# GpSimd adds the halves of each head before VectorE sums them in a softmax attention

## The chip, the cores and the metric

The kernel runs on one core of one Trainium2 chip. The metric is the device time of one execution in microseconds (us); lower is better. The engines are TensorE (PE; PEld is its weight load), VectorE (DVE), ScalarE (ACT), GpSimd (POOL) and SyncE (SP, here only a DMA queue). Each runs its own queue in order, and the queues meet at semaphores.

## The reference

Two attention layers, each followed by a feed-forward part with routed experts, on an input of 4 sequences of 512 rows of 256 values. The change lies in the second attention, a softmax over 64 keys in 16 heads:

```python
q = (Q @ Wq_w + Wq_b).reshape(b, tq, H, DK).transpose(0, 2, 1, 3)
scores = jnp.einsum('bhqd,bhkd->bhqk', q, k) / jnp.sqrt(jnp.float32(DK))
scores = jnp.where(mask == 0, jnp.float32(-1000000000.0), scores)
attn = jax.nn.softmax(scores, axis=-1)
out = jnp.einsum('bhqk,bhkd->bhqd', attn, v)
return out.transpose(0, 2, 1, 3).reshape(b, tq, c) @ Wo_w + Wo_b
```

Everything is float32. The layer norm ahead of it, and the routing and experts behind it, are part of the same kernel.

## The kernel before

The function `softmax_attention` runs from about 430 to 628 us of the span. The 2048 query rows are 16 tiles (n = 0 to 15) of 128 rows, four for each sequence b. One tile's scores are 128 x 1024 numbers (16 heads of 64 keys) in `s_sc`, a ring of three buffers. A hand-written schedule of 27 ticks sets the order on every engine; tick n works on these tiles:

- TensorE: `probs_T(n-2)` transposes the finished probabilities (L1045), then `scores(n+1)` (L50 to L52 with kz) computes the next scores, then what a remainder r = n mod 4 adds: the query projection `q_proj`, the output projection `project`, router logits, transposes of inputs.
- VectorE: `bounded(n)` copies the scores out of PSUM under the mask (L898) and takes each head's maximum (L904). Then `reciprocals(n-1)` sums the exponentials of each head (L910, 1024 columns to 16) and inverts the sums (L912). Then come the extras of r: layer-norm work (L877, L859 and the small chain of L83 to L88), low halves of the split numbers (L884, L890, L993), the residual (L917).
- GpSimd: its loop (L760 to L768) has in iteration n the subtraction of the maximum from tile n (L763), then the multiplication of tile n-1 by its reciprocals (L767).
- ScalarE: the exponential of tile n-1 (L829), the copy of the transposed tile n-2 (L835), and the extras of r: L794 (high half of the queries), L826 (high half of the attention output), L776 (layer norm), L787 (high half of a transposed input).

So the way of one tile n is: scores, L898, L904, L763, L829, L910, L912, L767, L1045, L835. In PE's queue, `scores(n+1)` stands behind `probs_T(n-2)`, and `bounded(n+1)` needs these scores and `probs_T(n-2)`. At tick 16 TensorE's queue holds `probs_T(14)`, `project(2)`, which waits for the transposed input of sequence 1 (L884, behind L787, behind L835), and from there on a row of products: the shared expert's first layer, logits, its second layer, and so on to about 628 us, where all engines leave the function together. Extras that are queued once a sequence on ScalarE stand ahead of the exponential when r is 1 or 3 (L794, L826).

Of the kernel before, what the change touches and what calls it, by code (L numbers as in the profile page):

```python
# [10 lines left out]
ALU = mybir.AluOpType  # L11
ACT = mybir.ActivationFunctionType
AX = mybir.AxisListType

B, S, D = 4, 512, 256
KEYS = 64
HEADS = 16
HD = D // HEADS
P = 128
T = B * S  # L20
NT = T // P
# [649 lines left out]
def softmax_attention(nc, k, io):  # L671
# [11 lines left out]
    with ctx:  # L683
        def sb(name, shape, dt=F32):
            return ctx.enter_context(nc.sbuf_tensor(f"s_{name}", shape, dt))

        def sem(name):
            return ctx.enter_context(nc.semaphore(f"s_{name}"))
# [14 lines left out]
        sc = sb("sc", [P, 3, HEADS, KEYS])  # L703
        top = sb("top", [P, 2, HEADS])
        pT = sb("pT", [P, PAIRS, S])
        den, rden = sb("den", [P, 2, HEADS]), sb("rden", [P, 2, HEADS])

        u32 = xq
# [9 lines left out]
        q_done, qh_ok, ql_ok = sem("q_done"), sem("qh_ok"), sem("ql_ok")  # L718
        s_done, cl_ok, mx_ok, sub_ok, p_ok, den_ok, sum_ok, nm_ok = (
            sem(n) for n in ("s_done", "cl_ok", "mx_ok", "sub_ok", "p_ok", "den_ok", "sum_ok", "nm_ok"))  # L720
        pt_done, pc_ok, pv_done, oh_ok, ol_ok = (sem(n) for n in ("pt_done", "pc_ok", "pv_done", "oh_ok", "ol_ok"))
        y_done, y_used, lg_done, lg_ok = (sem(n) for n in ("y_done", "y_used", "lg_done", "lg_ok"))
        fb_ld, f1_ld, f2_ld = sem("fb_ld"), [sem(f"f1_ld{h}") for h in range(2)], [sem(f"f2_ld{h}") for h in range(2)]
# [9 lines left out]
        @block.sync  # L733
        def _(sp):
            for h in range(2):
                sp.dma_start(f32(sw1_lo(h)), k["fw"][0, E1, :, h * FH:(h + 1) * FH]).then_inc(f1_ld[h], 16)
            sp.wait_ge(bo0, 1)
            sp.dma_start(bo[0:1, :], io["bo"]).then_inc(c_ld, 16)
            sp.dma_start(mask_i[:], io["mask"]).then_inc(c_ld, 16)
            sp.dma_start(rw[:], io["rw"][1]).then_inc(c_ld, 16)  # L740
            sp.dma_start(bq[:], io["bq"]).then_inc(fb_ld, 16)
            sp.dma_start(k["fb1"][:], io["fb1"]).then_inc(fb_ld, 16)

            sp.wait_ge(s_done, NT // 2)
            for h in range(2):
                sp.dma_start(f32(sw2_lo(h)), k["fw"][1, E1, :, h * FH:(h + 1) * FH]).then_inc(f2_ld[h], 16)

        @block.gpsimd
        def _(pool):
            def gather(b):  # L750
                for t in range(b * TB, (b + 1) * TB):
                    pool.indirect_dma_start(out=k["xn"][:, t, :], out_offset=None, in_=k["ys0"],
                                            in_offset=bass.IndirectOffsetOnAxis(ap=k["back0"][:, t:t + 1], axis=0)).then_inc(yg_ok[b], 16)

            gather(0)
            nc.gpsimd.memset(bo[:], 0.0).then_inc(bo0, 1)
            gather(1)
            gather(2)
            gather(3)
            for n in range(NT + 1):  # L760
                if n < NT:
                    pool.wait_ge(mx_ok, n + 1)
                    nc.gpsimd.tensor_tensor(sc[:, n % 3], sc[:, n % 3], top[:, n % 2, :, None].to_broadcast([P, HEADS, KEYS]),  # L763
                                            ALU.subtract).then_inc(sub_ok, 1)
                if 1 <= n < NT + 1:
                    pool.wait_ge(sum_ok, n)
                    nc.gpsimd.tensor_tensor(sc[:, (n - 1) % 3], sc[:, (n - 1) % 3],  # L767
                                            rden[:, (n - 1) % 2, :, None].to_broadcast([P, HEADS, KEYS]), ALU.mult).then_inc(nm_ok, 1)  # L768
# [86 lines left out]
        def _(dve):  # L855
# [48 lines left out]
                nc.vector.tensor_reduce(top[:, n % 2], sc[:, n % 3], AX.X, ALU.max).then_inc(mx_ok, 1)  # L904

            def reciprocals(n):
                dve.wait_ge(p_ok, n + 1)
                if n >= 2:
                    dve.wait_ge(nm_ok, n - 1)
                nc.vector.tensor_reduce(den[:, n % 2], sc[:, n % 3], AX.X, ALU.add).then_inc(den_ok, 1)  # L910
                dve.wait_ge(den_ok, n + 1)
                nc.vector.reciprocal(rden[:, n % 2], den[:, n % 2]).then_inc(sum_ok, 1)  # L912

# [53 lines left out]
            for n in range(TICKS):  # L967
# [3 lines left out]
                if 1 <= n < NT + 1:  # L971
                    reciprocals(n - 1)
# [1064 lines left out]
def build(nc, io, out):  # L2037
    ctx = ExitStack()
    with ctx:
# [45 lines left out]
        k["sw1_hi"], k["sw1_lo"] = (lambda h: sw1_hi[:, h]), (lambda h: sw1_lo[:, h])  # L2085
        k["sw2_hi"], k["sw2_lo"] = (lambda h: keys[:, B // 2 + h]), (lambda h: keys[:, h])
        softmax_attention(nc, k, io)
        last_ffn_phase(nc, k, io, out)

# [56 lines left out]
```

## Time and profile before

| | us |
|---|---|
| median of 3 runs | 827.67 (826.83 to 831.08) |
| the profiled execution | 825.63 |
| its span in the trace | 824.2 |

| engine | busy us | share of the span |
|---|---|---|
| TensorE (PE) | 670.3 | 81% |
| VectorE (DVE) | 524.8 | 64% |
| ScalarE (ACT) | 337.0 | 41% |
| GpSimd (POOL) | 209.0 | 25% |

Busy shares are averages over stages with different limits. In a timeline row the first two numbers are the start and the duration in us; the bracket, where there is one, is the idle time of that engine just before the instruction and what ended it.

### The profile page before, as it was taken

How to read it: one execution, taken by the hardware profiler on the slowest of the kernel's cores; microseconds unless marked ns; L12 is line 12 of the kernel's file. 1: busy time of each engine (PE TensorE's matmuls, PEld its weight loads, DVE VectorE, ACT ScalarE, POOL GpSimd, SP SyncE). 2: the span in 40 equal slices, each digit the busy share in tenths (PEclk: the TensorE clock that was granted, in tenths of full speed). 3: DMA queues.
4: the chain of work that ended last, by engine and by line, in shares of the span. 5: the costliest groups of instructions: out<-in, count | busy, mean ns of one | idle time of the engine just before them, and what ended most of it. 6: DMA issues, size and time to landing. Idle time of an engine off the chain costs nothing. (4 is left out here: it accounts for less than half of the span.)

```text
span 824.2 us, 15063 instructions
## 1 busy us (share of the span) xinstructions
PE 670.3 (81%) x4947; PEld 613.4 (74%) x4948; DVE 524.8 (64%) x1322; ACT 337.0 (41%) x555; POOL 209.0 (25%) x324
## 2 busy tenths in 40 slices
PE   4898825989999989998606578677897789999996
PEld 3566525889999989998505456457797789999995
DVE  6855645777445885447557888886545675565556
ACT  7544354554334563335522544444322433343321
POOL 7533250000000000000063565550001711011161
PEclk9999956999999999999857779898998999999998
DMA  7999126655100449200141001000004411111124
GB/s 268 419 417 392 74 94 242 210 159 177 59 25 25 137 176 358 92 25 13 33 128 32 1 0 52 1 0 1 1 1 151 168 48 38 39 51 51 35 74 135
DMA packets 22997, 90.71 MB, mean 110 GB/s; under 512 B 4401, under 2 KB 8754, under 8 KB 17362
## 3 DMA queue, kind: packets, MB, share of 16 engines
q1 hardware_dynamic: 15794, 68.64, 22.4%
q0 software_dynamic: 7168, 21.63, 8.7%
q8 instruction: 18, 0.29, 0.1%
q14 instruction: 17, 0.14, 0.1%
HBM read 50.94 MB, written 45.61 MB: 117 GB/s over the span
## 5 line engine op out<-in xcount | busy, mean ns | idle before, releaser
L1469 ACT ACTIVATE e_h<-psum,e_be 128x256 f32<-128x256 f32 x144 | 67.7, 475 | 141.8 <-PE psum L52 140.2
L50 PE MATMUL psum<-e_h_hi,e_w_hi 128*128 128x256 f32 x384 | 110.2, 287 | 6.2 <-DVE e_w_lo L1560 5.5
L51 PE MATMUL psum<-e_h_lo,e_w_hi 128*128 128x256 f32 x384 | 107.9, 281 | 0.0
L52 PE MATMUL psum<-e_h_hi,e_w_lo 128*128 128x256 f32 x384 | 107.8, 281 | 0.0
L1866 ACT ACTIVATE vz<-psum,fb 128x256 f32<-128x256 f32 x112 | 52.4, 474 | 108.3 <-PE psum L52 105.0
L1552 DVE CAST e_h_hi<-e_h 128x256 fp32r<-128x256 f32 x144 | 43.5, 302 | 82.6 <-ACT e_h L1469 82.6
L50 PEld LDWEIGHTS psum<-e_h_hi,e_w_hi 128*128 128x128 f32 x384 | 72.3, 188 | 9.7 <-DVE e_w_lo L1560 8.8
L52 PEld LDWEIGHTS psum<-e_h_hi,e_w_lo 128*128 128x128 f32 x384 | 72.4, 188 | 0.0
L51 PEld LDWEIGHTS psum<-e_h_lo,e_w_hi 128*128 128x128 f32 x384 | 72.3, 188 | 0.0
L1554 DVE TENSOR_TENSOR e_h_lo<-e_h,e_h_hi 128x256 fp32r<-128x256 f32 x144 | 61.3, 426 | 4.9
L50 PE MATMUL psum<-e_gT_hi,e_w_hi 128*128 128x256 f32 x192 | 55.5, 289 | 9.4 <-DVE e_w_lo L1627 7.8
L52 PE MATMUL psum<-e_gT_hi,e_w_lo 128*128 128x256 f32 x192 | 54.7, 285 | 0.0
L51 PE MATMUL psum<-e_gT_lo,e_w_hi 128*128 128x256 f32 x192 | 54.7, 285 | 0.0
L1915 DVE TENSOR_TENSOR f_h_lo<-vz,f_h_hi 128x256 fp32r<-128x256 f32 x112 | 47.7, 426 | 3.8
L50 PEld LDWEIGHTS psum<-e_gT_hi,e_w_hi 128*128 128x128 f32 x192 | 37.1, 193 | 10.8 <-issue 10.8
L1913 DVE CAST f_h_hi<-vz 128x256 fp32r<-128x256 f32 x112 | 33.2, 297 | 17.7 <-ACT vz L1866 16.4
L763 POOL TENSOR_TENSOR s_sc<-s_sc,s_top 128x1024 f32<-128x1024 f32 x16 | 30.4, 1903 | 55.0 <-DVE s_top L904 54.9
L50 PE MATMUL psum<-kz_hi,s_qT_hi 128*128 128x256 f32 (+1 forms) x80 | 32.5, 407 | 13.8 <-DVE s_sc L898 9.8
L50 PE MATMUL psum<-f_gT_hi,f_w_hi 128*128 128x256 f32 x144 | 40.2, 279 | 0.0
L50 PE MATMUL psum<-xT_hi,sw_hi 128*128 128x256 f32 (+1 forms) x128 | 38.2, 298 | 2.5 <-issue 1.3
L51 PE MATMUL psum<-f_gT_lo,f_w_hi 128*128 128x256 f32 x144 | 40.2, 279 | 0.0
L52 PE MATMUL psum<-f_gT_hi,f_w_lo 128*128 128x256 f32 x144 | 40.2, 279 | 0.0
(410 smaller groups left out, 2129.8 us busy)
## 6 DMA issues: line engine op xcount, KB each, us to landing
xs<-zeros SPq DMA_DIRECT2D x18, 1024.0 KB
e_w_raw<-in_W SPq DMA_DIRECT2D x18, 1024.0 KB, 5.2
ys<-zeros SPq DMA_DIRECT2D x6, 1024.0 KB
ys<-e_yo POOLq DMA_DIRECT2D x14, 256.0 KB, 3.7
e_xg<-xs POOLq DMA_DIRECT2D x13, 256.0 KB, 6.8
e_w_raw<-in_W SPq DMA_DIRECT2D x6, 512.0 KB, 8.0
f_w_lo<-fw SPq DMA_DIRECT2D x6, 512.0 KB
ys<-x_norm POOLq DMA_DIRECT2D x10, 256.0 KB, 2.6
```

What stands on the lines that cost most here:

```text
L50: nc.tensor.matmul(out, wh, xh, start=start, stop=False)
L51: nc.tensor.matmul(out, wh, xl, start=False, stop=False)
L52: return nc.tensor.matmul(out, wl, xh, start=False, stop=stop)
L763: nc.gpsimd.tensor_tensor(sc[:, n % 3], sc[:, n % 3], top[:, n % 2, :, None].to_broadcast([P, HEADS, KEYS]), ALU.subtract).then_inc(sub_ok, 1)
L1469: nc.scalar.activation(h32[:, m % RING], ps[:, HIDDEN_BANKS[m % RING], 0:SLOT], ACT.Gelu, bias=be[:, m:m + 1]).then_inc(gelu_ok, 1)
L1552: nc.vector.tensor_copy(h_hi[:, m], h32[:, m % RING]).then_inc(hh_ok, 1)
L1554: nc.vector.tensor_tensor(h_lo[:, m], h32[:, m % RING], f32(h_hi[:, m]), ALU.subtract).then_inc(hl_ok, 1)
L1866: nc.scalar.activation(h32[:, m % RING], ps[:, HIDDEN_BANKS[m % RING], 0:SLOT], ACT.Relu, bias=b1[:, f * MH + m:f * MH + m + 1]).then_inc( ...
L1913: nc.vector.tensor_copy(h_hi[:, m], h32[:, m % RING]).then_inc(hh_ok, 1)
L1915: nc.vector.tensor_tensor(h_lo[:, m], h32[:, m % RING], f32(h_hi[:, m]), ALU.subtract).then_inc(hl_ok, 1)
```

## The change

A buffer `pairs` (128 x 16 x 32) and a semaphore `add_ok` are new. In the GpSimd loop, iteration n first waits for the exponential of tile n-1 and adds the two halves of 32 keys of each head into `pairs` (512 columns out of twice 512); from n = 2 on it also waits until VectorE has read `pairs` of the tile before (`den_ok`). Only then come the subtraction of tile n and the multiplication of tile n-1, as before. VectorE's sum waits for that addition in place of the exponential, and reads 512 columns of `pairs` in place of 1024 of `s_sc`.

```diff
+        pairs = sb("pairs", [P, HEADS, KEYS // 2])
...
+        add_ok = sem("add_ok")
...
             for n in range(NT + 1):
+
+                if 1 <= n < NT + 1:
+                    pool.wait_ge(p_ok, n)
+                    if n >= 2:
+                        pool.wait_ge(den_ok, n - 1)
+                    p = sc[:, (n - 1) % 3]
+                    nc.gpsimd.tensor_tensor(pairs[:], p[:, :, 0:KEYS // 2], p[:, :, KEYS // 2:KEYS], ALU.add).then_inc(add_ok, 1)
                 if n < NT:
                     pool.wait_ge(mx_ok, n + 1)
                     nc.gpsimd.tensor_tensor(sc[:, n % 3], sc[:, n % 3], top[:, n % 2, :, None].to_broadcast([P, HEADS, KEYS]),
...
             def reciprocals(n):
-                dve.wait_ge(p_ok, n + 1)
+                dve.wait_ge(add_ok, n + 1)
                 if n >= 2:
                     dve.wait_ge(nm_ok, n - 1)
-                nc.vector.tensor_reduce(den[:, n % 2], sc[:, n % 3], AX.X, ALU.add).then_inc(den_ok, 1)
+                nc.vector.tensor_reduce(den[:, n % 2], pairs[:], AX.X, ALU.add).then_inc(den_ok, 1)
```

## Rows read from the trace of the kernel before

**Rows 1.** The page, busy us, share of the span and instruction count of each engine:

```profile
PE 670.3 (81%) x4947; PEld 613.4 (74%) x4948; DVE 524.8 (64%) x1322; ACT 337.0 (41%) x555; POOL 209.0 (25%) x324
```

**Rows 2.** Stretches of the span: length, busy us of PE, PEld, DVE, ACT, POOL; clock; DMA:

```profile
440.00:560.00 120.00, 83.84 (x432) 62.37 (x430) 100.11 (x180) 54.75 (x69) 61.34 (x32) 0.83 0.03 9
560.00:628.00 68.00, 60.87 (x464) 57.97 (x464) 36.15 (x106) 20.41 (x37) 0.00 (x0) 0.92 0.00 1
```

**Rows 3.** Groups in 440 to 560 us: busy us, mean ns | idle before, its releasers:

```profile
L898 DVE SCALAR_TENSOR_TENSOR s_sc<-psum,s_cap 128x1024 f32<-128x1024 f32 x16 | 19.5, 1222 | 7.5 <-PE psum L52 7.4
L910 DVE TENSOR_REDUCE s_den<-s_sc 128x16 f32<-128x1024 f32 x16 | 19.4, 1210 | 4.2 <-ACT s_sc L829 4.2
...
L767 POOL TENSOR_TENSOR s_sc<-s_sc,s_rden 128x1024 f32<-128x1024 f32 x16 | 31.4, 1965 | 4.0 <-DVE s_rden L912 4.0
L763 POOL TENSOR_TENSOR s_sc<-s_sc,s_top 128x1024 f32<-128x1024 f32 x16 | 30.4, 1903 | 55.0 <-DVE s_top L904 54.9
```

**Rows 4.** Groups of the whole span that have nearby sizes, same columns:

```profile
L1608 DVE TENSOR_REDUCE e_r_gone<-e_r_after 128x16 f32<-128x128 f32 x1 | 0.3, 288 | 0.0
...
L66 POOL TENSOR_TENSOR a_ln_tmp<-a_ln_tmp,a_ln_half 128x4 f32<-128x4 f32 x9 | 1.8, 199 | 0.7
...
L1442 POOL MEMSET e_yo<- 128x512 f32 x1 | 0.5, 522 | 0.0
```

**Rows 5.** Timeline, ticks 1 to 3, VectorE, TensorE and GpSimd:

```profile
459.81 1.21 DVE L910 TENSOR_REDUCE s_den<-s_sc 128x16 f32<-128x1024 f32 x1
459.98 1.90 POOL L763 TENSOR_TENSOR s_sc<-s_sc,s_top 128x1024 f32<-128x1024 f32 x1 [8.10 <-DVE s_top L904]
...
461.84 1.90 POOL L767 TENSOR_TENSOR s_sc<-s_sc,s_rden 128x1024 f32<-128x1024 f32 x1
...
462.46 1.21 DVE L898 SCALAR_TENSOR_TENSOR s_sc<-psum,s_cap 128x1024 f32<-128x1024 f32 x1
...
463.79 1.97 PE L1045 MATMUL psum<-ident,s_sc 128*128 128x128 f32 x8 [2.17 <-POOL s_sc L767]
...
468.36 1.22 DVE L898 SCALAR_TENSOR_TENSOR s_sc<-psum,s_cap 128x1024 f32<-128x1024 f32 x1 [2.02 <-PE psum L52]
```

**Rows 6.** Timeline, ticks 9 and 10, GpSimd, ScalarE and VectorE:

```profile
507.05 1.91 POOL L763 TENSOR_TENSOR s_sc<-s_sc,s_top 128x1024 f32<-128x1024 f32 x1
...
507.95 1.27 ACT L794 ACTIVATE s_qT_hi<-psum,s_bq 128x512 fp32r<-128x512 f32 x2 [4.82 <-PE psum L52]
509.11 1.06 ACT L829 ACTIVATE s_sc<-s_sc 128x1024 f32<-128x1024 f32 x1
...
510.20 1.22 DVE L910 TENSOR_REDUCE s_den<-s_sc 128x16 f32<-128x1024 f32 x1 [3.23 <-ACT s_sc L829]
...
513.50 1.05 ACT L829 ACTIVATE s_sc<-s_sc 128x1024 f32<-128x1024 f32 x1
```

**Rows 7.** Timeline, ticks 15 and 16, from the last exponentials to `project(2)`:

```profile
551.32 1.05 ACT L829 ACTIVATE s_sc<-s_sc 128x1024 f32<-128x1024 f32 x1
551.48 1.90 POOL L763 TENSOR_TENSOR s_sc<-s_sc,s_top 128x1024 f32<-128x1024 f32 x1 [1.24 <-DVE s_top L904]
...
552.40 1.22 DVE L910 TENSOR_REDUCE s_den<-s_sc 128x16 f32<-128x1024 f32 x1 [0.99 <-ACT s_sc L829]
...
553.98 1.90 POOL L767 TENSOR_TENSOR s_sc<-s_sc,s_rden 128x1024 f32<-128x1024 f32 x1 [0.60 <-DVE s_rden L912]
...
555.94 1.09 PE L1045 MATMUL psum<-ident,s_sc 128*128 128x128 f32 x8 [3.68 <-POOL s_sc L767]
...
557.99 1.02 ACT L787 ACTIVATE xT_hi<-psum 128x1024 fp32r<-128x1024 f32 x1
...
559.04 1.23 DVE L884 TENSOR_TENSOR xT_lo<-psum,xT_hi 128x1024 fp32r<-128x1024 f32 x1 [2.65 <-ACT xT_hi L787]
...
560.37 0.55 PE L50 MATMUL psum<-s_w_hi,s_oT_hi 128*128 128x256 f32 x1 [3.33 <-issue]
```

**Rows 8.** Timeline, GpSimd's one long multiplication:

```profile
477.65 2.88 POOL L767 TENSOR_TENSOR s_sc<-s_sc,s_rden 128x1024 f32<-128x1024 f32 x1
```

## The prediction

> **What bounds the kernel now.** I read the page first: TensorE is busy for 81% of the span, VectorE 64%, GpSimd 25% [rows 1]. These averages hide the stage that is touched, so next came the stretches [rows 2]. From 440 to 560 us, where the 16 softmax tiles run, VectorE is busy 100.1 of 120 us, TensorE 83.8 and GpSimd 61.3. From 560 to 628 us, the rest of the function, VectorE has 36 of 68 us and TensorE 60.9. So only the first stretch can pay for less VectorE work, and it pays only up to the instruction that opens the second: `project(2)` on TensorE at 560.37 [rows 7]. From there TensorE's queue runs one fixed row of products with short waits, and all engines leave together, so a shift of that start passes on one for one.
>
> Inside the stretch the groups tell who makes VectorE wait [rows 3]: 7.4 us before its L898 for scores from TensorE, and 4.2 us before its L910 for the exponential. GpSimd stood idle for 55 us before its subtractions, waiting for VectorE's maximum, and 4.0 us before its multiplications. It looks like a free engine beside a full one. The timeline has to say where each is late.
>
> **The change part by part.** The sum is walked through the queues: each instruction starts at the later of its queue coming free and its last input being done plus 0.03 us; durations are those of the trace. For the kernel before, this walk lands `project(2)` at 560.18, where the trace has 560.37, so it is good to about 0.2 us; differences are better.
>
> *The shorter sum.* L910 takes 1210 ns for 1024 columns [rows 3], and a reduction of 128 columns into 16 takes 288 ns [rows 4]. The slope is (1210 - 288) / 896 = 1.03 ns a column, so 512 columns take 288 + 384 x 1.03 = 683 ns. VectorE saves 0.53 us a tile, 8.5 us over 16 tiles. The bound from the other side is no saving at all (the fixed cost or the layout eats it).
>
> *The added addition.* No row shows this operation. GpSimd's two-input operation takes 199 ns for 4 columns [rows 4] and 1903 ns for 1024 [rows 3]: slope 1.67 ns, so 512 columns take 199 + 508 x 1.67 = 1048 ns. I take 1.05 us. From below, a memset of 512 columns, which reads nothing, takes 0.52 us [rows 4]; from above, the subtraction of 1024 columns takes 1.90 us, since both halves together are 1024 numbers read and the large row reads one of its operands broadcast. The row nearest in kind and form is the two-input operation, hence the value from its slope.
>
> The Trainium skill, "GPSIMD Engine Reference", section "Elementwise — side-by-side cycle accounting", gives 4497 ns for a two-input add of 2048 columns; a quarter of it is an estimate of 1.12 us, and with it the sum below would end 0.2 us later. The same page's section on engine selection says to leave elementwise work and sums along the free dimension to VectorE. By it the move costs more than it frees, and the rows here agree (1.05 us spent for 0.53 us freed); whether that shows in the time depends on who is waiting.
>
> *The moved waits.* The addition stands at the head of the iteration, so behind its wait for the exponential of tile n-1 are queued the subtraction of tile n (for which the exponential n waits on ScalarE, and through it everything after) and the multiplication n-1 (for which TensorE waits). The wait for `den_ok` of the tile before costs nothing: that sum is over before the multiplication that stands ahead in GpSimd's own queue.
>
> Now tick by tick, times against before:
>
> - Ticks 1 to 3. `bounded(2)` at 462.46 follows back to back behind the sum of 459.81 and comes 0.53 earlier. `bounded(3)` at 468.36 waited 2.02 us for TensorE, whose queue had `probs_T(0)` first, which waited for the multiplication of tile 0 [rows 5]. That multiplication starts when the subtraction gives GpSimd free (459.98, then 461.84, 1.86 later), so it does not move, and neither does `bounded(3)`. Gain 0.
> - Ticks 4 to 8. VectorE is the late one at ticks 5 and 6: `bounded(5)` comes 0.51 earlier and `bounded(6)` 1.04. From there TensorE's scores set the pace, moved by the same. GpSimd's iteration is now 1.01 + 1.86 + 1.86 = 4.73 us, against some 3.4 of VectorE in a tick without extras (L898, L904 and the sum at 1.22, 1.22 and 0.68, and a short inversion), and just fits in ticks that have extras or a wait for scores. Gain 1.1 at `bounded(8)`.
> - Ticks 9 and 10. ScalarE has L794 ahead of the exponential of tile 8, at 509.11, and VectorE waits 3.23 us for it [rows 6]. All this comes 1.08 earlier, but the addition (1.05 + 0.03) stands between: the sum starts at 510.21, where it was. Only its own 0.53 is left as gain. The subtraction of tile 9, at 507.05 before [rows 6], now starts at 510.1; its exponential ran only at 513.50 [rows 6], behind other work of ScalarE, which covers this delay of 3 us; were that cover gone, tick 10 would be 3 us later.
> - Ticks 11 to 15. Nothing more is won, since scores and extras set the pace: `bounded(15)` and the exponential of tile 14 come 0.53 earlier.
> - The exit. The exponential of tile 14 ends at 552.37 in the trace [rows 7], now at 551.84. The addition runs 551.87 to 552.92. Before, the subtraction of tile 15 ran from 551.48, beside this exponential; now it stands behind the addition and starts at 552.88. The multiplication of tile 14 waits for GpSimd and starts at 552.88 + 1.86 = 554.74, though its reciprocal is ready at about 553.9. Before, it started at 553.98 [rows 7]: 0.76 later. Behind it come L1045, L835, L787, L884 and `project(2)`, each released by the one before [rows 7], with nothing to absorb the delay.
>
> Sum: 0.53 earlier turned into 0.8 later (0.81 in the walk) at `project(2)`. The profiled execution (825.63, 1.4 us more than its span of 824.2) would go to 826.4, and the median of 827.67 to **828.5**.
>
> Bounds in the same walk: an addition of 0.52 us gives -0.3; 1.27 us gives +1.6; 1.90 us gives +4.9. An unshortened sum with the addition of 1.05 gives +2.6.
>
> **The rivals.**
>
> *GpSimd becomes the loop (slower).* If the addition costs near the large row's 1.90 us, GpSimd's iteration is 3 x 1.86 = 5.6 us. Then the add and subtraction are late in the ticks around 5, 10, 12 and 13 too, and the walk ends 4.9 us later: 832.6. It decides from about 1.1 us on: up to there only the exit is lost, above it each further 0.1 us costs 0.4 to 0.5. For it: both inputs are full tensors, unlike any row. One multiplication took 2.88 in place of 1.90 us, beside VectorE's L877 [rows 8], so a neighbour can stretch GpSimd. Against it: L877 runs twice in all, and no addition falls beside it. The skill's page "GPSIMD Engine Reference", section "Specifications", names VectorE instructions with two SBUF inputs as contenders, and L877 is one; by it the additions, which lie beside others, would not be stretched.
>
> *The gain stays (faster).* If TensorE's scores were early in most ticks, 0.53 would be kept in each: 8.5 less the 1.3 lost at the exit, 7.2 us faster, 820.5. For it: VectorE is busy 83% of the stretch. Against it: the waits of [rows 3] and the two places above where nothing is kept.
>
> *The sum does not get shorter.* Then 1.21 us of VectorE stays, and the time is 827.67 + 2.6 = 830.3.
>
> *The clock.* TensorE's granted clock averages 0.83 in the first stretch and 0.92 in the second [rows 2], so stretches at 1.2 GHz lie among those at 2.4 GHz. In the second, which is TensorE's, 0.92 means 2 x 0.08 x 68 = 10.9 us at the lower level. The shift can make that a third more or less: 3.6 us at half speed, 1.8 us of time either way, at this size still within 0.5%.
>
> **How the numbers follow.** The forecast has 0.75 (no change that can be measured; about 0.5%, 4.1 us, is what a measurement of this kernel can tell from none), GpSimd as the loop 0.09 (slower), the gain that stays 0.05 (faster), the unshortened sum 0.03 (no change), the clock by more than 1.8 us 0.08 (0.01 faster, 0.02 slower, the rest no change). That makes 0.06 faster, 0.83 the same, 0.11 slower. The range reaches down by the clock and the short addition to 826.0, and up to the dear addition, 832.6.
>
> **What would show each step.** The sum at L910's place near 0.68 us; the new addition near 1.05 us and 16 times; `bounded(3)` unmoved; the subtraction of tile 9 about 3 us later with nothing waiting; VectorE's idle time before its sum grown, released by GpSimd; at the exit the order addition, subtraction, multiplication back to back, and `project(2)` 0.8 us later. An addition above 1.3 us, or scores that arrive early in ticks 3 and 11 to 15, would make the prediction wrong.

## The result, and the profile after

The changed kernel takes 839.12 us (median of 4 executions, 837.94 to 841.33) against 828.04 for the kernel before in the same comparison: ratio 1.0126, 95% interval 1.0092 to 1.016, so 11.1 us slower. Forecast was 828.5, no change that can be measured, in a range of 826.0 to 832.6. The profiled execution took 841.33 us and has a span of 839.9.

The stretches say where the time went. The cuts lie at four events: the first L898 of tile 0 (L907 in the changed kernel), the start of `project(2)`, the end of the function's last logits, and the first transposed routed slot of the next function. First the kernel before, then the changed one; the columns are those of rows 2.

```profile
447.40:560.37 112.97, 79.50 (x423) 59.39 (x421) 95.43 (x168) 51.90 (x63) 61.34 (x32) 0.83 0.03 10
560.37:628.20 67.83, 61.07 (x464) 58.05 (x464) 35.78 (x105) 20.04 (x37) 0.00 (x0) 0.92 0.00 1
628.20:673.52 45.32, 34.48 (x247) 32.49 (x247) 32.31 (x81) 15.42 (x26) 22.54 (x36) 0.89 0.46 166
673.52:824.20 150.68, 141.38 (x1190) 139.51 (x1188) 87.79 (x243) 50.27 (x105) 28.69 (x34) 0.99 0.19 58
```

```profile
450.06:568.14 118.08, 83.57 (x422) 63.95 (x421) 89.84 (x168) 52.02 (x63) 80.89 (x48) 0.79 0.03 10
568.14:641.39 73.25, 66.49 (x464) 63.45 (x464) 35.75 (x105) 20.09 (x37) 0.00 (x0) 0.85 0.00 1
641.39:689.38 47.99, 34.47 (x247) 32.55 (x247) 32.32 (x81) 15.07 (x26) 20.76 (x36) 0.86 0.43 157
689.38:839.90 150.52, 140.66 (x1190) 139.65 (x1188) 88.18 (x243) 50.45 (x105) 28.81 (x34) 0.99 0.19 58
```

The 16 ticks take 5.1 us more. The part behind `project(2)` takes 5.4 us more with the same 464 matmuls: TensorE's busy time there grows by all of it (61.07 to 66.49 us, with 6.76 us idle in both), and its granted clock is 0.85 in place of 0.92. The next function takes 2.7 us more and the part ahead of the ticks 2.7 us (450.06 against 447.40); neither holds changed code, and the first experiment takes both out.

Inside the ticks, the groups that answer to rows 3 (busy us, mean ns | idle before, its releasers):

```profile
L776 POOL TENSOR_TENSOR s_sc<-s_sc,s_rden 128x1024 f32<-128x1024 f32 x16 | 31.5, 1967 | 1.1 <-DVE s_rden L921 1.1
L772 POOL TENSOR_TENSOR s_sc<-s_sc,s_top 128x1024 f32<-128x1024 f32 x16 | 30.5, 1906 | 28.5 <-DVE s_top L913 28.5
L769 POOL TENSOR_TENSOR s_pairs<-s_sc 128x512 f32<-128x512 f32 x16 | 20.4, 1274 | 16.1 <-ACT s_sc L838 16.1
...
L907 DVE SCALAR_TENSOR_TENSOR s_sc<-psum,s_cap 128x1024 f32<-128x1024 f32 x16 | 19.5, 1221 | 8.8 <-PE psum L52 8.6
...
L919 DVE TENSOR_REDUCE s_den<-s_pairs 128x16 f32<-128x512 f32 x16 | 10.9, 682 | 12.5 <-POOL s_pairs L769 12.3
```

VectorE's sum fell from 1210 to 682 ns, as worked out (683). That frees 8.5 us, but VectorE now waits 12.3 us for the addition, where it waited 4.2 us for the exponential [rows 3]. The addition takes 1.27 us, not 1.05, and GpSimd itself waits 16.1 us for exponentials with the next subtraction queued behind.

Tick 0 shows something the prediction did not have (timeline of VectorE and of GpSimd):

```profile
459.09 0.16 DVE L87 SCALAR_TENSOR_TENSOR s_ln_rstd<-s_ln_tmp,s_ln_rstd 128x4 f32<-128x4 f32 x1
459.29 1.10 DVE L85 TENSOR_TENSOR s_ln_tmp<-s_ln_rstd 128x4 f32<-128x4 f32 x1
460.43 0.16 DVE L86 TENSOR_TENSOR s_ln_tmp<-s_ln_tmp,s_ln_half 128x4 f32<-128x4 f32 x1
...
459.12 1.25 POOL L769 TENSOR_TENSOR s_pairs<-s_sc 128x512 f32<-128x512 f32 x1 [4.59 <-ACT s_sc L838]
```

One operation of 4 columns in the layer-norm chain takes 1.10 us in place of 0.16, and ends 0.02 us after the addition beside it. In tick 13 the same happens to an operation with one input, 1.04 us in place of 0.17. In that tick VectorE also waits 2.12 us for `project(1)`, where it waited 0.33 before; `project(1)` begins at 538.20, and from there TensorE has no pause until tile 15's scores are done at 554.45:

```profile
546.68 1.27 POOL L769 TENSOR_TENSOR s_pairs<-s_sc 128x512 f32<-128x512 f32 x1 [2.32 <-ACT s_sc L838]
546.93 1.04 DVE L875 TENSOR_SCALAR s_ln_var<-s_ln_mv 128x4 f32<-128x4 f32 x1
...
543.76 1.28 DVE L926 SCALAR_TENSOR_TENSOR x_res<-psum,tg,x_res 128x1024 f32<-128x1024 f32 x1 [2.12 <-PE psum L1074]
...
538.20 0.35 PE L50 MATMUL psum<-s_w_hi,s_oT_hi 128*128 128x256 f32 x1 [1.94 <-issue]
```

The tick that answers to rows 6 (ScalarE, GpSimd, VectorE) and the exit that answers to rows 7:

```profile
512.12 1.06 ACT L838 ACTIVATE s_sc<-s_sc 128x1024 f32<-128x1024 f32 x1
513.25 1.28 POOL L769 TENSOR_TENSOR s_pairs<-s_sc 128x512 f32<-128x512 f32 x1 [3.50 <-ACT s_sc L838]
514.49 1.90 POOL L772 TENSOR_TENSOR s_sc<-s_sc,s_top 128x1024 f32<-128x1024 f32 x1
514.57 0.69 DVE L919 TENSOR_REDUCE s_den<-s_pairs 128x16 f32<-128x512 f32 x1 [4.44 <-POOL s_pairs L769]
...
556.84 1.04 ACT L838 ACTIVATE s_sc<-s_sc 128x1024 f32<-128x1024 f32 x1
557.96 1.27 POOL L769 TENSOR_TENSOR s_pairs<-s_sc 128x512 f32<-128x512 f32 x1 [1.25 <-ACT s_sc L838]
559.19 1.91 POOL L772 TENSOR_TENSOR s_sc<-s_sc,s_top 128x1024 f32<-128x1024 f32 x1
559.27 0.69 DVE L919 TENSOR_REDUCE s_den<-s_pairs 128x16 f32<-128x512 f32 x1 [2.29 <-POOL s_pairs L769]
559.99 0.25 DVE L921 RECIPROCAL s_rden<-s_den 128x16 f32<-128x16 f32 x1
...
561.05 1.90 POOL L776 TENSOR_TENSOR s_sc<-s_sc,s_rden 128x1024 f32<-128x1024 f32 x1
...
563.01 1.80 PE L1054 MATMUL psum<-ident,s_sc 128*128 128x128 f32 x8 [2.81 <-POOL s_sc L776]
568.14 0.55 PE L50 MATMUL psum<-s_w_hi,s_oT_hi 128*128 128x256 f32 x1 [3.33 <-issue]
```

The queue order is the forecast one: addition, subtraction, multiplication, back to back, with the reciprocal ready at 560.24, 0.8 us before GpSimd takes it.

Counted from tile 0's L898, these are the starts of the L898 of some tiles, and of `project(2)`:

| | tile 1 | 2 | 3 | 6 | 9 | 10 | 12 | 14 | 15 | project(2) |
|---|---|---|---|---|---|---|---|---|---|---|
| before | 10.02 | 15.06 | 20.96 | 40.88 | 57.09 | 71.20 | 81.00 | 96.52 | 101.52 | 112.97 |
| changed | 10.96 | 15.47 | 21.57 | 41.05 | 57.59 | 72.38 | 83.01 | 100.32 | 104.43 | 118.08 |
| difference | +0.94 | +0.41 | +0.61 | +0.17 | +0.50 | +1.18 | +2.01 | +3.80 | +2.91 | +5.11 |

### The profile page after: what moved, and what is told of

It is laid out like the page before. It is cut to its first block and busy times, and to the rows that moved or that the text cites. A ratio compares the mean times of both kernels' runs of the same rounds, so it can differ in the third digit from the quotient of the medians.

```text
span 839.9 us, 15094 instructions
## 1 busy us (share of the span) xinstructions
PE 681.5 (81%) x4947; PEld 626.4 (75%) x4948; DVE 519.1 (62%) x1322; ACT 337.1 (40%) x555; POOL 227.2 (27%) x340
## 5 line engine op out<-in xcount | busy, mean ns | idle before, releaser
L1478 ACT ACTIVATE e_h<-psum,e_be 128x256 f32<-128x256 f32 x144 | 67.8, 475 | 141.9 <-PE psum L52 140.3
L50 PE MATMUL psum<-e_h_hi,e_w_hi 128*128 128x256 f32 x384 | 110.3, 287 | 6.2 <-DVE e_w_lo L1569 5.5
L50 PEld LDWEIGHTS psum<-e_h_hi,e_w_hi 128*128 128x128 f32 x384 | 72.3, 188 | 9.7 <-DVE e_w_lo L1569 8.8
L50 PE MATMUL psum<-e_gT_hi,e_w_hi 128*128 128x256 f32 x192 | 55.5, 289 | 9.4 <-DVE e_w_lo L1636 7.8
L50 PE MATMUL psum<-kz_hi,s_qT_hi 128*128 128x256 f32 (+1 forms) x80 | 33.6, 420 | 15.6 <-DVE s_sc L907 11.5
L50 PEld LDWEIGHTS psum<-e_gT_hi,e_w_hi 128*128 128x128 f32 x192 | 37.2, 194 | 10.8 <-issue 10.8
L50 PE MATMUL psum<-f_gT_hi,f_w_hi 128*128 128x256 f32 x144 | 40.2, 279 | 0.0
L50 PE MATMUL psum<-xT_hi,sw_hi 128*128 128x256 f32 (+1 forms) x128 | 37.9, 296 | 1.1 <-issue 1.1
```

What stands on the lines that cost most here:

```text
L50: nc.tensor.matmul(out, wh, xh, start=start, stop=False)
L1478: nc.scalar.activation(h32[:, m % RING], ps[:, HIDDEN_BANKS[m % RING], 0:SLOT], ACT.Gelu, bias=be[:, m:m + 1]).then_inc(gelu_ok, 1)
```

## The experiments

Each time is given as a ratio to the kernel before, timed beside it on the same chip, with its 95% interval, since the kernel before itself has medians from 822.4 to 828.0 us in these comparisons. "Ticks" is the stretch from the first L898 to `project(2)`, "behind" the stretch from there to the function's end; 113.0 and 67.8 in the kernel before.

**Both kernels again.** No edit. Are the parts outside the ticks the change's?

> The kernel before once more, unchanged, for a second profile of it. The change as the cause of everything: bounded(0) again near 447.4 us, 113.0 us from there to project(2), 67.8 us from there to the end of the function, granted clock 0.92, total within 2 us of 828. Chance as the cause of the parts outside the 16 ticks (in the changed kernel's profile 2.7 us before the first tile, 5.5 us behind project(2) and 2.7 us in the next function): one of these parts comes out longer here too, by 2 us or more.

> The changed kernel once more, unchanged. If its queues are the cause: 118.0 us again from bounded(0) to project(2), within 0.5, and the 5.5 us behind project(2) again, since the same idle stretch of TensorE is ahead of it; 2.7 us before the first tile gone if that was chance. If the clock of TensorE falls by chance: behind project(2) anything between 68 and 74 us.

The kernel before again: ratio 1.0006 (0.9986 to 1.0027), ticks 112.99, behind 67.85. The changed kernel again: 1.0132 (1.0093 to 1.017), ticks 118.07, behind 73.81, next function 43.2 us in both. So the next function's 2.7 us were chance. The first tile starts anywhere from 447.3 to 451.7 us over 16 profiles of kernels of either kind (451.7 in one without any addition), so that difference is chance too. The 5.1 and the 5.4 to 6.0 us repeat, and together are the 11 us.

**The gain alone.** VectorE sums 512 columns of a constant tile, no addition.

```diff
-nc.vector.tensor_reduce(den[:, n % 2], sc[:, n % 3], AX.X, ALU.add)
+nc.vector.tensor_reduce(den[:, n % 2], pairs[:], AX.X, ALU.add)   # kernel before; pairs is filled once with 1.0
```

> Leaves out the addition on GpSimd: VectorE sums 512 columns of a constant tile in place of the 1024 exponentials of a tile, with the waits of the kernel before, so the probabilities are not normalised. It is the gain alone. The walk through the queues: bounded(6) 1.1 us earlier, bounded(10) 1.6 us, project(2) 2.2 us earlier: 110.8 us for the stretch, and the total 2 us below before (0.3 per cent). The rival, that VectorE's busy time is the bound and 16 x 0.53 us are worth their full 8.5 us: 819.5 us.

Ratio 0.9976 (0.9954 to 0.9999), ticks 109.8: 3.2 us off the ticks and 2.1 us off the median. The walk had 2.2. The rest is TensorE's clock: its product of the probabilities with the values behind the scores of tile 6 took 2.83 us in place of 3.64, and `q_proj` behind those of tile 9 took 2.74 in place of 3.67. So 8.5 us of VectorE's time were worth 3.2 here, even at no cost.

**The cost alone.** The addition as in the changed kernel, but VectorE sums the 1024 columns and waits for the exponential; GpSimd waits for its own additions, which keeps `s_sc` safe.

```diff
-pool.wait_ge(den_ok, n - 1)
+pool.wait_ge(add_ok, n - 1)
...
+pool.wait_ge(add_ok, n)        # ahead of the multiplication
...
-dve.wait_ge(add_ok, n + 1)
+dve.wait_ge(p_ok, n + 1)
...
-nc.vector.tensor_reduce(den[:, n % 2], pairs[:], AX.X, ALU.add)
+nc.vector.tensor_reduce(den[:, n % 2], sc[:, n % 3], AX.X, ALU.add)
```

> The addition runs on GpSimd as in the changed kernel, but nobody uses it: VectorE sums the 1024 exponentials itself and does not wait for the addition. It is the cost alone. If an addition of 1.27 us only fills GpSimd's queue: the walk gives project(2) 1.7 us later (114.7 us for the stretch). If besides it shuts VectorE out of small two-input operations while it runs, as one of them that took 1.10 instead of 0.16 us in the profile of the changed kernel suggests: 1 us more for each of the layer-norm chains that an addition meets (two of them there), 116.5 us. The total 3 to 9 us above before, the rest of it TensorE's clock.

> The kernel with an addition that nobody uses, unchanged. Its profiled execution took 824.7 and its four timed ones 834.6 to 836.4. If the clock behind project(2) has two outcomes for the same instructions, this profile may show the other: stretch 116.3 again, and 73 to 79 us behind project(2) in an execution of 835. If the stretch itself differs by 5 us or more, the two outcomes lie inside the 16 ticks.

Ticks 116.3 and 115.6. The walk had 114.7 for the queue alone and 116.5 with two waits of the kind seen in tick 0 (the lock, see below), so the first profile is near the second value and the other one midway. The first tick takes 10.96 in both, that is, 0.94 longer, though no one waits for the addition. Ratios 1.0157 (1.0121 to 1.0193) and 1.0082 (1.0047 to 1.0117): the executions of these identical kernels spread from 822.7 to 836.4 us. Both profiles are of quick ones (824.7 and 822.7) with 67.9 and 68.2 behind, so which stretch holds the 10 us of the others was not seen.

**The form of the addition, and the lock.** A kernel of its own: GpSimd runs an operation twice, alone or beside 20 VectorE operations of 4 columns (or 5 sums of 512, or 4 copies of 256).

> A kernel of its own that leaves out the whole computation: it copies its input to its output, and beside that GpSimd runs pairs of one operation alone, then beside small VectorE operations. Form of the addition: if the strided halves are the cause of 1.27 us, the flat 512-column addition takes about 1.05; if two full operands are, all of them take 1.27 and the one with a broadcast operand about 1.05. Lock: if a GpSimd operation with two inputs shuts out VectorE operations with two SBUF inputs until it ends, some 128x4 operations of VectorE show up to 1.3 us in place of 0.16 beside the additions, and none beside a GpSimd memset or where VectorE reads one input, or one from PSUM. If it is a plain share of bandwidth, all kinds get a little longer and none waits for the end.

GpSimd's groups (busy us, mean ns; L38 is the addition of strided halves, L42 flat operands, L45 and L53 a broadcast second operand, L50 two full ones):

```profile
L38 POOL TENSOR_TENSOR g_o<-g_a 128x512 f32<-128x512 f32 x12 | 14.9, 1261 | 7.4 <-DVEq L115 7.1
...
L53 POOL TENSOR_TENSOR g_o<-g_a,g_s 128x1024 f32<-128x1024 f32 x4 | 7.5, 1906 | 0.3
...
L50 POOL TENSOR_TENSOR g_o<-g_a,g_b 128x1024 f32<-128x1024 f32 x2 | 4.6, 2337 | 0.1
...
L42 POOL TENSOR_TENSOR g_o<-g_a,g_b 128x512 f32<-128x512 f32 x2 | 2.5, 1260 | 0.1
L45 POOL TENSOR_TENSOR g_o<-g_a,g_s 128x512 f32<-128x512 f32 x2 | 2.0, 1046 | 0.1
```

The form of the halves costs nothing (1261 against 1260). The broadcast operand is what made the large row cheap: 512 columns with one take 1046 ns, which is to 2 ns the price that the prediction took from such a row.

VectorE's operations (count, then minimum / median / maximum ns): beside additions, two SBUF inputs (L68), one SBUF input (L71), one from PSUM (L74), sums of 512 (L77), copies of 256 (L81); then L68 again beside a GpSimd operation with one input, beside a memset, and beside the broadcast subtraction:

```profile
L68 DVE TENSOR_TENSOR v_o<-v_a x20: 146/151/1264, 24.1 to 29.8; 128x4 f32<-128x4 f32 x20
L71 DVE TENSOR_SCALAR v_o<-v_a x20: 151/152/1227, 29.8 to 33.3; 128x4 f32<-128x4 f32 x20
L74 DVE TENSOR_TENSOR v_o<-psum,v_a x20: 141/142/146, 33.4 to 34.7; 128x4 f32<-128x4 f32 x20
L77 DVE TENSOR_REDUCE v_o<-v_a x5: 666/668/671, 34.8 to 37.1; 128x16 f32<-128x512 f32 x5
L81 DVE COPY v_w<-v_a x4: 281/770/1337, 37.7 to 39.5; 128x256 f32<-128x256 f32 x4
L68 DVE TENSOR_TENSOR v_o<-v_a x20: 147/148/150, 40.6 to 42.0; 128x4 f32<-128x4 f32 x20
L68 DVE TENSOR_TENSOR v_o<-v_a x20: 149/152/161, 45.1 to 46.5; 128x4 f32<-128x4 f32 x20
L68 DVE TENSOR_TENSOR v_o<-v_a x20: 149/151/1869, 47.1 to 51.9; 128x4 f32<-128x4 f32 x20
```

So it is a lock, held by a whole GpSimd instruction: beside one with two inputs, a small VectorE operation waits up to its full 1.26 or 1.87 us, and the others run at their usual speed. It hits VectorE operations on SBUF with two inputs, and with one input too where they are of the scalar kind or a copy, which was not expected. It spares the sums and the operations with an operand in PSUM (11 of those 20 met an addition). GpSimd operations with one input or none did not hold up the two-input ones (161 ns at most). One copy took 1.12 us beside a one-input GpSimd operation without ending with it, which stays open. The Trainium skill, "SBUF — State Buffer", section "SBUF: two separate sides", says that the port pair shared by the two engines is an "exclusive lock" for the whole instruction of whichever starts first. The trace agrees for two-input GpSimd instructions. The page counts every GpSimd operation that reads SBUF against a two-input one of VectorE; here the one with a single input (2798 ns) held up none.

**Parts undone.** Tiles named in WHOLE are summed whole by VectorE, without an addition:

```diff
+WHOLE = (0, 13)                 # x4; (14, 15) x1; all of 0 to 13 x5; (0, 8, 12, 14, 15) x2; (0, 8, 13, 14, 15) x3
-                if 1 <= n < NT + 1:
+                if 1 <= n < NT + 1 and n - 1 not in WHOLE:
...
+                if n in WHOLE:
+                    dve.wait_ge(p_ok, n + 1)
```

> The changed kernel with tiles 0 and 13 summed whole by VectorE: these are the two additions that ran beside a layer-norm chain (the expectation of the run before called the second one tile 12, which was the wrong tile). If the lock is the cause: tick 0 is 0.94 us shorter (10.0 us to bounded(1)), tick 13 0.87 us shorter, less the longer sums of 0.53 each; stretch 117.0 us. If not, 118.1 plus 0.5 to 1 for the longer sums.

> The changed kernel with tiles 14 and 15 summed whole by VectorE, as before, without an addition. The exit alone is undone: the walk with an addition of 1.27 us takes 1.6 us off the stretch (116.4 us). If the clock's answer depends on the stretch, the part behind project(2) may be 67.9 or 73 us, so a total of 827 or 832.

> The kernel before with the addition for the last two tiles only (14 and 15). The walk gives the exit alone: the sum of tile 14 waits for the addition (1.27 us, less 0.53), the subtraction of tile 15 stands behind it; stretch 115.0 us (2.0 more than 113.0). If these two additions alone draw the clock loss behind project(2), that part takes 73 us and the total is 7 to 8 us above before; if it needs the lateness of the ticks ahead too, 67.9 and 2 us.

> The changed kernel with tiles 0, 8, 12, 14 and 15 summed whole by VectorE: without the two additions that met a layer-norm chain (tiles 0 and 12), the one behind the late exponential (8) and the exit. The walk gives project(2) 0.7 us earlier than in the kernel before; with VectorE's 0.3 at L877 lost, 112.6 us for the stretch, and with the clock as in before a total within 1 us of it. If something else than these places costs the 5.1 us, the stretch stays above 115.

> The changed kernel with tiles 0, 8, 13, 14 and 15 summed whole by VectorE: the hybrid before with tile 13 in place of 12, so that neither layer-norm chain meets an addition. The lock takes 0.9 us off its 113.5: 112.6 us, 0.4 below before. Total within 1 us of before if the part behind project(2) takes 67.9, 3 us above if it takes 70.9 as in the last hybrid.

| | ticks | behind | ratio (interval) |
|---|---|---|---|
| changed kernel, both profiles | 118.1, 118.1 | 73.3, 73.8 | 1.0126, 1.0132 |
| x4, without tiles 0 and 13 | 115.9 | 68.3 | 1.0063 (1.004 to 1.0085) |
| x1, without the exit | 115.3 | 68.3 | 1.0043 (1.0023 to 1.0063) |
| x5, the exit alone | 115.4 | 68.3 | 1.0057 (1.003 to 1.0085) |
| x2, first hybrid | 113.5 | 70.9 | 1.0024 (1.0003 to 1.0045) |
| x3, second hybrid | 113.5 | 70.9 | 1.0026 (1.0004 to 1.0048) |

x4: tick 0 takes 10.02 and tick 13 9.95 us, as before, where the changed kernel has 10.96 and 12.37. The lock is 0.9 of each; the other 1.5 us of tick 13 are `project(1)`, which ran partly at the lower clock in the changed kernel, VectorE waiting 2.1 us for it. x5: the exit costs 2.4 us by itself (2.0 expected, 1.3 forecast); 0.9 of it is `probs_T(14)` at the lower clock (1.97 us against 1.09). x1 takes 2.8 us off (1.6 expected). The hybrids keep 0.5 us more than the kernel before has, not the 0.4 to 0.7 less that the walk gave. The first of them undid the wrong tile (its tick 13 has the lock, 10.84 us); the second has not (9.96), but the 0.9 is gone by the L898 of tile 15, 101.93 in the one and 101.94 in the other, which waits for its scores in both.

Neither is free of the lock, nor is x4. With tile 0's addition gone, the work of tick 4 lies otherwise, and tile 4's addition meets the layer-norm chain there, as in no kernel with tile 0's addition. Tick 4 (from L898 of tile 4 to that of tile 5) takes 11.03 us in x2, x3 and x4, against 10.00 in the kernel before and 10.01 in the changed one. In x3:

```profile
482.66 1.26 POOL L770 TENSOR_TENSOR s_pairs<-s_sc 128x512 f32<-128x512 f32 x1 [1.05 <-ACT s_sc L839]
482.75 1.19 DVE L88 SCALAR_TENSOR_TENSOR s_ln_rstd<-s_ln_tmp,s_ln_rstd 128x4 f32<-128x4 f32 x1
```

These 1.0 us are about what the hybrids lack against the walk. A hybrid that sums tile 4 whole too was not run, so it is not shown that none can beat the kernel before; what there is to win is near the 0.24% of the gain alone.

**Delays alone.** Unused sums of 1024 columns on VectorE, `pad` being a tile of ones; in the kernel before (d1, d4) or the changed one (x6, x7):

```diff
+                for i in range({14: 2}.get(n, 0)):      # d1; 4 in d4, 1 in x6, 3 in x7
+                    nc.vector.tensor_reduce(padded[:, i], pad[:], AX.X, ALU.add)
                 if n < NT:
                     bounded(n)
...
+                for i in range(8, 8 + (4 if n == NT else 0)):     # d1; 5 in d4, none in x6 and x7
+                    nc.vector.tensor_reduce(padded[:, i], pad[:], AX.X, ALU.add)
```

> The kernel before with VectorE work that nobody uses: 2 sums of 1024 columns (2.3 us) ahead of bounded(14) and 4 (4.5 us, of which 2.6 fall into an idle stretch) ahead of the transposed input that opens project(2). No GpSimd work is added. Stretch 117.1 us (113.0 + 2.3 + 1.9). If the 5.5 us lost behind project(2) are the clock's answer to a late and thinner TensorE queue, they come here too: 73 us from project(2) to the end of the function and a total of 832 to 834. If they are GpSimd's doing, the part behind stays at 67.9 and the total at 827.

> The kernel before with VectorE work that nobody uses: 4 sums of 1024 columns ahead of bounded(14) and 5 ahead of the transposed input that opens project(2), no work on GpSimd. About as late as the changed kernel: stretch 118.0 us (113.0 + 3.4 + 1.6 by what the smaller delay gave). If lateness of TensorE's queue alone draws the clock loss behind project(2), that part takes 73 to 74 us, as in both profiles of the changed kernel, and the total is 11 us above before. If it takes 67.8 to 68.3, as with the smaller delay, lateness alone is not enough and the total is 5 us above before.

> The changed kernel with 1 more sum of 1024 columns on VectorE, unused, ahead of bounded(14): everything from there 1.1 us later, stretch 119.2. If the clock loss behind project(2) hangs on how the work lies to the clock's falls, a shift of 1 us may end it (68 us) and the total falls by 4 us although work was added. If it is a fixed consequence of the additions, 73.5 us and 1.1 us more in total (12.5 above before).

> The same with 3 more sums: 3.4 us later, stretch 121.5. Fixed consequence: 73.5 us behind project(2) and 3.4 us more in total than the changed kernel (14.5 above before). Alignment: 68 to 71 us behind, and a total of 8.5 to 11 above before.

| | ticks | behind | median us, that of before beside it | ratio (interval) |
|---|---|---|---|---|
| d1 | 115.5 | 68.3 | 831.38, 827.35 | 1.0051 (1.0028 to 1.0075) |
| d4 | 119.7 | 67.9 | 831.02, 823.43 | 1.0101 (1.0068 to 1.0134) |
| x6 | 117.6 | 73.7 | 833.37, 822.41 | 1.0137 (1.0106 to 1.0168) |
| x7 | 119.1 | 68.1 | 828.83, 822.41 | 1.0085 (1.006 to 1.0111) |

None of the four reaches `project(2)` when it was expected to (117.1, 118.0, 119.2 and 121.5). In x6 the delay is hidden again by the L898 of tile 15, which waits for its scores (104.41 us, and 104.43 in the changed kernel), so x6 is nearly the changed kernel once more.

d4 is 1.6 us later at `project(2)` than the changed kernel, and loses nothing behind. So lateness alone does not draw the loss. x6 and x7 differ by two unused sums on VectorE; the one with more work is 4.5 us faster on the same chip (seven of its eight times lie below all four of x6). Both, with ticks and behind:

```profile
449.03:566.65 117.62, 80.71 (x421) 61.86 (x420) 91.12 (x169) 52.04 (x63) 80.91 (x48) 0.82 0.03 10
566.65:640.33 73.68, 66.92 (x464) 63.89 (x464) 35.74 (x105) 20.07 (x37) 0.00 (x0) 0.85 0.00 1
```

```profile
450.05:569.18 119.13, 81.86 (x421) 62.71 (x420) 93.40 (x171) 52.15 (x63) 80.87 (x48) 0.80 0.03 9
569.18:637.25 68.07, 61.30 (x464) 58.31 (x464) 35.79 (x105) 20.08 (x37) 0.00 (x0) 0.92 0.00 1
```

A part of it shows in the five us around the logits (`s_rw`, 24 matmuls of 2 columns), x6 first, then x7:

```profile
582.00:587.00 5.00, 5.00 (x27) 5.00 (x27) 3.80 (x22) 0.85 (x2) 0.00 (x0) 0.54 0.00 0
```

```profile
583.20:588.00 4.80, 4.45 (x34) 4.45 (x35) 4.25 (x23) 0.03 (x1) 0.00 (x0) 0.87 0.00 0
```

In x6 (as in the changed kernel, clock 0.57 in 583 to 588) the granted clock is down to 1.2 GHz while most of the logits run, which take 4.7 us in place of 2.8; in x7 and in the kernel before it falls only when they are done. The next logits, 30 us on, take 4.45 us in x6 and 2.84 in x7. The rest of the 5.6 us lies in the other matmuls under these falls, and in `project(2)` itself: there the lower clock, with which it starts in all of these kernels, lasts 5.5 us in x6 and 3.9 in x7 (5.3 in the changed kernel, 3.4 in the kernel before).

## Why the prediction was wrong, step by step

It forecast no change and named the right place, the exit, and the right engine. Four steps failed, two of them terms of the sum.

- *Price of the addition, 1.05 us.* It takes 1.27. The slope came from a row with a broadcast operand, which costs less for each column. The upper bound of 1.90 was taken from that row too, and held. With 1.27 the prediction's own walk gives +1.6 at `project(2)`.
- *"No addition falls beside it."* The neighbour was taken for a source of stretched GpSimd operations, and only L877 was looked at, so the sum has nothing for VectorE waiting on an addition. The lock works both ways, and it hits the small layer-norm operations as well. The trace of before had both directions: the long multiplication of 2.88 us [rows 8] is its usual 1.90 and a wait for L877, and the L877 of tick 0, beside a subtraction, took 2.02 us where the two ahead of it took 1.28 (rows below the list). The lock cost 0.9 us in each of ticks 0 and 13, shown by x4. That of tick 0 would account for 0.9 of the 1.3 us missing at tile 8 (1.1 earlier forecast, 0.16 later measured). That of tick 13 does not reach `project(2)`: TensorE, without a pause from `project(1)` on, sets the start of tile 15's L898 and, through ScalarE's copies, that of tile 14's exponential.
- *The exit, 1.3 us.* Its order was right, and it adds 2.2 in the changed kernel (13.65 from L898 of tile 15 to `project(2)` against 11.45), 2.4 alone (x5). The dear addition gives 0.2 of the difference; `probs_T(14)` at the lower clock gives the rest (1.80 against 1.09 [rows 7]).
- *The clock, nothing in the sum, 1.8 us either way, with 0.08 for more.* It is over half of the result: 5.4 to 6.0 us behind `project(2)`, and about 2 us within the ticks (`project(1)`, `probs_T(14)`). The price was a third more or less of the 10.9 us at the lower level. Worked out the same way, the changed kernel has 2 x 0.15 x 73 = 22 us there, twice as much. What counts is which work lies under a fall, and a shift of the schedule can decide it (x6 against x7).

The rows of tick 0 in the kernel before (GpSimd's subtraction ends at 451.87):

```profile
449.97 1.90 POOL L763 TENSOR_TENSOR s_sc<-s_sc,s_top 128x1024 f32<-128x1024 f32 x1 [11.94 <-DVE s_top L904]
450.93 2.02 DVE L877 SCALAR_TENSOR_TENSOR x_res<-x_norm,tg,x_res 128x1024 f32<-128x1024 f32 x1
```

The lower end of the range was also added up wrong: by the clock and the short addition it is 827.67 - 0.3 - 1.8 = 825.6, not 826.0.

Right were: the shorter sum (683 forecast, 682 measured); `bounded(2)` 0.53 earlier (+0.94 turns to +0.41); the subtraction of tile 9 far later with nothing waiting; the tile-8 addition eating the gain (+0.50 turns to +1.18 between tiles 9 and 10, forecast 0.55, measured 0.68); and the rival that VectorE's 8.5 us would all be gained, which fell with 0.05 (k3: 3.2 at no cost). The rival on GpSimd as the loop had the right sign, by the price of 1.90 us, which was not the cause.

The sum now, for the ticks: walk with 1.27 us +1.6, the lock of tick 0 +0.9, the clock in `project(1)` +1.5 and in `probs_T(14)` +0.7, together 4.7 of the 5.1. The parts overlap, so this is no exact account. Behind: +5.4, clock. What stays open: why the changed kernel's timing draws the loss in each of its two profiles, whether it is the same loss that makes some executions of k4 and k5 some 10 us longer, and what fixes the moment of a fall.

## What to carry to other kernels

Price an operation from a row with the same kind of operands, not only the same engine: a broadcast operand alone moved this one by 20%. Before giving GpSimd two-input work, list VectorE's SBUF operations that can meet it, small ones above all: each can wait for the whole GpSimd instruction. Look again after each edit, since taking one addition out moved the meeting to another tick. And when the granted clock of a TensorE stage lies between its two levels, as here (0.85 and 0.92), a shift of a few us in the work ahead can cost or give back 5 us, so compare stage lengths and granted clock over repeated profiles, and try a pure delay, before a cause is named.

## What the runs showed of the hardware that was not expected

- GpSimd, 512 columns: 1260 ns with two full operands, 1046 with one of them broadcast; 1024 columns: 2337 and 1906. One input (tensor_scalar) is dearer still: 1490 ns for 512 and 2798 for 1024.
- VectorE operations on SBUF with a single input (tensor_scalar, copy) wait for a two-input GpSimd instruction too (taking up to 1.23 and 1.34 us in all); sums do not. A one-input GpSimd instruction, though longer, held up no two-input VectorE operation.
- Two kernels that differ by two unused VectorE sums (2.3 us of work) stand 4.5 us apart the other way, by the granted clock of one stretch (0.85 against 0.92).
